# Four decoder layers on one core: expert products in groups of four within 8 steps of a scan, its lead 24 steps instead of 32, and the masks and scatters of a retrieval's tile 0 between its last picks

## What is computed

```python
# layer 1
h_new = (1-z)*n + z*h                      # GRU, 256 steps
base_out = h @ W_base.T + b_base           # _L1_ffn_ref
expert_idx = argmax(softmax(h @ router_W.T))
delta = ((h @ A) * onehot) @ Bw
x = x + base_out + delta * SCALING
# layer 2: drive = x
i_couple = tanh(q) @ coupling.T            # four times a step, each from the one before
q_next, p_next = _rk4_step(q, p, drive, coupling, bias)
# retrieval, per token, 8 heads, 8 of 4096 experts each
z = einsum('btd,bthkd->bthk', h, down_embed[indices])
z = silu(z * softmax(sc))
out = einsum('bthk,bthkd->btd', z, up_embed[indices])
x = x + out
```

## Time and profile before

| | |
|---|---|
| median of 3 runs | 5199.05 us (5195.85 to 5218.25) |
| profiled execution | 5227.58 us, span 5225.8 us |
| TensorE busy | 4851.0 us, 93% of the span |
| VectorE busy | 2831.0 us, 54% |
| ScalarE busy | 1520.9 us, 29% |
| GpSimd busy | 280.7 us, 5% |
| scan | about 966 to 2990 us of the span |
| retrieve_experts | about 2990 to 4410 us |

### The profile page before, as it was taken

How to read it: one execution, slowest core, us unless ns; L and a number is a source line. 1 busy time by engine, 2 the same in 40 slices (tenths; PEclk the granted TensorE clock), 3 DMA queues, 4 the chain that set the end, 5 groups by cost and what they waited for, 6 DMA issues and landing times. The chain is left out here.

```text
span 5225.8 us, 196853 instructions
## 1 busy us (share of the span) xinstructions
PE 4851.0 (93%) x83712; PEld 3836.6 (73%) x83712; DVE 2831.0 (54%) x16413; ACT 1520.9 (29%) x6006; POOL 280.7 (5%) x859
## 2 busy tenths in 40 slices
PE   7899999799999999999996699999989998999978
PEld 3344654589999999999996588799889997344433
DVE  3211011379999999999997635675544341444411
ACT  1100111234444444444443223233322221333310
POOL 0010010001111111111111000000000000000000
PEclk7699999655555555555555599999989999899989
DMA  2201431000000000000001000033400000000000
GB/s 80 101 34 41 165 140 35 14 4 5 5 5 5 5 5 5 5 5 5 5 5 51 13 9 2 34 87 93 128 14 3 3 3 34 11 16 17 12 21 32
DMA packets 54335, 163.72 MB, mean 31 GB/s; under 512 B 13873, under 2 KB 18097, under 8 KB 48192
## 3 DMA queue, kind: packets, MB, share of 16 engines
q1 hardware_dynamic: 47456, 134.89, 7.7%
q0 software_dynamic: 3712, 12.29, 0.7%
q10 hardware_dynamic: 2304, 4.20, 0.2%
HBM read 129.63 MB, written 17.17 MB: 28 GB/s over the span
## 5 line engine op out<-in xcount | busy, mean ns | idle before, releaser
L616 PE MATMUL k_ps<-k_hl,k_wlo 128*128 128x8 f16 x16384 | 606.6, 169 | 141.0 <-ACT k_hl L692 135.9
L616 PEld LDWEIGHTS k_ps<-k_hl,k_wlo 128*128 128x128 f16 x16384 | 532.9, 105 | 178.2 <-ACT k_hl L692 160.6
L620 PE MATMUL k_ps<-k_hl,k_whi 128*128 128x16 f16 x16384 | 588.6, 174 | 0.0
L620 PEld LDWEIGHTS k_ps<-k_hl,k_whi 128*128 128x128 f16 x16384 | 516.1, 104 | 0.6
L616 PE MATMUL g_ps<-g_hl,g_wlo 128*128 128x8 f16 x12288 | 436.7, 168 | 43.2 <-DVE g_hl L770 38.2
L620 PE MATMUL g_ps<-g_hl,g_whi 128*128 128x16 f16 x12288 | 441.5, 174 | 0.0
L616 PEld LDWEIGHTS g_ps<-g_hl,g_wlo 128*128 128x128 f16 x12288 | 387.1, 104 | 49.4 <-DVE g_hl L770 43.6
L692 ACT ACTIVATE k_hl<-k_q 128x32 f16<-128x32 f32 x768 | 176.2, 229 | 742.9 <-DVE k_q L727 742.9
L620 PEld LDWEIGHTS g_ps<-g_hl,g_whi 128*128 128x128 f16 x12288 | 387.1, 104 | 0.0
L1441 DVE TENSOR_REDUCE t_NM<-t_ps 128x1 f32<-128x512 f32 x256 | 165.1, 686 | 218.2 <-PE t_ps L1310 218.2
L1213 DVE TENSOR_TENSOR HQ<-p_ior,p_pm 128x2048 f32<-128x2048 f32 x64 | 146.3, 2290 | 223.7 <-PE p_sim L1037 223.7
(11 more groups left out here) (326 smaller groups left out, 8960.7 us busy)
## 6 DMA issues: line engine op xcount, KB each, us to landing
GRZ<-expert_places SPq DMA_DIRECT2D x64, 512.0 KB, 4.9
wm<-in_w_dram SPq DMA_DIRECT2D x4, 2816.0 KB, 10.4
GRZ<-in_w_dram SPq DMA_DIRECT2D x4, 2816.0 KB, 9.8
m_w<-in_w2a_dram SPq DMA_DIRECT2D x8, 1280.0 KB, 12.7
GRZ<-in_ue_dram SPq DMA_DIRECT2D x8, 1024.0 KB, 8.4
XT<-in_xT_dram SPq DMA_DIRECT2D x1, 4096.0 KB, 12.5
GRZ<-in_x_nat_dram SPq DMA_DIRECT2D x4, 1024.0 KB, 18.8
expert_rows<-wm SPq DMA_DIRECT2D x1, 4096.0 KB, 23.7
```

Of the source, the lines that this page charges most:

```text
L616: T.matmul(P[:,j,1,:],lo[:,kc,(m0+j)*128:(m0+j+1)*128],x[:,kc,0,:],start=(j==0 and kc==0),stop=False,skip_group_check=True)
L620: i=T.matmul(P[:,j,:,:],hi[:,kc,(m0+j)*128:(m0+j+1)*128],x[:,kc,:,:],start=False,stop=kc==KC-1,skip_group_check=True)
```

## The change

In `scan`, LEAD becomes 24. The expert work of a chunk lies in the steps i = 0 to 7: all four products with 136 columns at i = 0, four base products a step at i = 1 to 4, the transposition at i = 2, the mask at i = 3, the four low-rank products at i = 5, the additions at i = 6 and 7. NE is TL*NB, still 128, so sizes don't change. In `retrieve_experts`, the weights of tile 0 are built behind pick tile 12, its first mask behind tile 13, its other three between the products of tile 15, in buffers of their own (B0: parts of wm, R and HF). Its scatters stand behind the picks of tile 15, and ScalarE's copies of them too. The masks of tile 1 come in the order 1, 2, 3, 0, then its weights. In the last phase, combine (0,q) now stands ahead of scatter (1,q); from tile 1 on the order is as before.

```diff
-LEAD, TL = 32, 16
+LEAD, TL = 24, 16
...
-                if i<2:
-                    if i==0:
-                        e.wait_ge(g_h,TL*(j+1))
-                        if j==0: e.wait_ge(s_lw,64)
-                    for d in (2*i,2*i+1):
-                        x=T.matmul(psh[:,0:136],hs[:,d,:],ar[:,d,:],start=d==0,stop=d==3)
-                    if i==1: x.then_inc(l_h,1)
-                if i==2: e.wait_ge(l_x,4*j)
-                if 2<=i<10:
-                    for u in (2*(i-2),2*(i-2)+1):
-                        dc,d=u//4,u%4
-                        T.matmul(pso[:,dc*128:(dc+1)*128],wb[:,d,dc*128:(dc+1)*128],hs[:,d,:],start=u==0,stop=False,skip_group_check=True)
-                if i==4:
+                if i==0:
+                    e.wait_ge(g_h,TL*(j+1))
+                    if j==0: e.wait_ge(s_lw,64)
+                    for d in range(4):
+                        x=T.matmul(psh[0:NE,0:136],hs[:,d,:],ar[:,d,:],start=d==0,stop=d==3)
+                    x.then_inc(l_h,1)
+                if i==1: e.wait_ge(l_x,4*j)
+                if 1<=i<5:
+                    dc=i-1
+                    for d in range(4):
+                        T.matmul(pso[:,dc*NE:(dc+1)*NE],wb[:,d,dc*128:(dc+1)*128],hs[:,d,:],start=dc==0 and d==0,stop=False,skip_group_check=True)
+                if i==2:
                     e.wait_ge(l_ht,j+1)
...
-                if i in (10,11):
+                if i==5:
...
-                if i!=5 or j<0 or j>=NT//TL: return
+                if i!=3 or j<0 or j>=NT//TL: return
...
-                elif i in (12,13):
-                    dc=2*(i-12)+part
+                elif i in (6,7):
+                    dc=2*(i-6)+part
...
+        B0=[x.rearrange('p (j r) -> p j r',r=128) for x in (wm[:,4096:6144],R[:,0:2048],R[:,2048:4096],HF[:,0:2048])]
...
                     dense(i+1,2*q)
                     pick(i,q)
                     dense(i+1,2*q+1)
+                    if i==NTL-1: scatter(0,q)
...
-            for q in range(4): scatter(0,q)
             for i in range(NTL):
                 for q in range(4):
-                    scatter(i+1,q)
+                    if i>=1: scatter(i+1,q)
                     combine(i,q)
+                    if i==0: scatter(1,q)
...
                     if q==1 and i>=1: weight(i-1)
+                    if i==NTL-1: spread(0,q)
...
-                if i>=1: e.wait_ge(s_W,n-3)
-                else: e.wait_ge(s_t,4*NTL-3+q)
+                if i==0 and q>=1: e.wait_ge(s_t,4*NTL-3)
+                if i==1: e.wait_ge(s_t,4*NTL)
+                if i==1 and q==0: e.wait_ge(s_W,4)
+                if i>=2: e.wait_ge(s_W,n-3)
...
                     rows_hot(4*i+4+q)
+                    if i==NTL-1 and q<3: pairs_hot(q+1)
...
-            for q in range(4): pairs_hot(q)
-            weights_hot(0)
-            for q in range(3): pairs_hot(4+q)
+                if i==NTL-4: weights_hot(0)
+                if i==NTL-3: pairs_hot(0)
+            for q in range(1,4): pairs_hot(4+q)
+            pairs_hot(4)
             weights_hot(1)
-            pairs_hot(7)
```

More of the change, by code:

```diff
@@ L591, in scan @@
         view=lambda P: P[:,0:64].rearrange('p (m s b) -> p s m b',m=KC,s=2)
-        R_,Z_,N_=range(3)
+        R_,Z_,N_=range(3); NE=TL*NB
         a,h=DT/2,DT
@@ L632, in experts @@
                 hs=HS[:,j%2].rearrange('p d t b -> p d (t b)')
-                if i<2:
-                    if i==0:
-                        e.wait_ge(g_h,TL*(j+1))
-                        if j==0: e.wait_ge(s_lw,64)
-                    for d in (2*i,2*i+1):
-                        x=T.matmul(psh[:,0:136],hs[:,d,:],ar[:,d,:],start=d==0,stop=d==3)
-                    if i==1: x.then_inc(l_h,1)
-                if i==2: e.wait_ge(l_x,4*j)
-                if 2<=i<10:
-                    for u in (2*(i-2),2*(i-2)+1):
-                        dc,d=u//4,u%4
-                        T.matmul(pso[:,dc*128:(dc+1)*128],wb[:,d,dc*128:(dc+1)*128],hs[:,d,:],start=u==0,stop=False,skip_group_check=True)
-                if i==4:
+                if i==0:
[10 more added lines that the diff above has]
+                if i==2:
                     e.wait_ge(l_ht,j+1)
-                    T.transpose(pst[:,0:128],ht[:],K.ident[:]).then_inc(l_tr,1)
-                if i in (10,11):
+                    T.transpose(pst[:,0:NE],ht[0:NE,:],K.ident[0:NE,0:NE]).then_inc(l_tr,1)
+                if i==5:
                     e.wait_ge(l_hm,j+1)
-                    for dc in (2*(i-10),2*(i-10)+1):
-                        x=T.matmul(pso[:,dc*128:(dc+1)*128],bw[:,dc*128:(dc+1)*128],hm[:],start=False,stop=True,skip_group_check=True)
-                    if i==11: x.then_inc(l_o,1)
+                    for dc in range(4):
+                        x=T.matmul(pso[:,dc*NE:(dc+1)*NE],bw[:,dc*128:(dc+1)*128],hm[:,0:NE],start=False,stop=True,skip_group_check=True)
+                    x.then_inc(l_o,1)
             for s in range(LEAD):
@@ L680, in masked @@
                 j,i=s//TL-1,s%TL
-                if i!=5 or j<0 or j>=NT//TL: return
-                e.wait_ge(l_tr,j+1); A.activation(hm[:],pst[:,0:128],ACT.Copy,scale=2.0).then_inc(l_hm,1)
+                if i!=3 or j<0 or j>=NT//TL: return
+                e.wait_ge(l_tr,j+1); A.activation(hm[:,0:NE],pst[:,0:NE],ACT.Copy,scale=2.0).then_inc(l_hm,1)
             scaled(0)
@@ L777, in experts @@
                 if j<0 or j>=NT//TL: return
-                if i==2 and part==0:
+                if i==1 and part==0:
                     e.wait_ge(l_h,j+1)
-                    at['mx']=ch.did(V.tensor_reduce(mx[:],psh[:,128:136],AX.X,ALU.max))
-                elif i==2:
[L782 to L787, removed]
+                    at['mx']=ch.did(V.tensor_reduce(mx[0:NE,:],psh[0:NE,128:136],AX.X,ALU.max))
+                elif i==1:
+                    ch.after(at['mx'])
+                    at['mk']=ch.did(V.scalar_tensor_tensor(mk[0:NE,:],psh[0:NE,128:136],mx[0:NE,0:1],io[0:NE,:],ALU.is_ge,ALU.mult))
+                elif i==2 and part==0:
+                    ch.after(at['mk'])
+                    at['ix']=ch.did(V.tensor_reduce(ix[0:NE,:],mk[0:NE,:],AX.X,ALU.min))
+                elif i==2:
                     ch.after(at['ix'])
-                    V.scalar_tensor_tensor(ht[:],io16[:],ix[:,0:1],psh[:,0:128],ALU.is_equal,ALU.mult).then_inc(l_ht,1)
-                elif i in (12,13):
-                    dc=2*(i-12)+part
+                    V.scalar_tensor_tensor(ht[0:NE,:],io16[0:NE,:],ix[0:NE,0:1],psh[0:NE,0:128],ALU.is_equal,ALU.mult).then_inc(l_ht,1)
+                elif i in (6,7):
+                    dc=2*(i-6)+part
                     e.wait_ge(l_o,j+1)
                     x=XT[:,dc,:,j*TL:(j+1)*TL].rearrange('p b t -> p t b')
-                    V.scalar_tensor_tensor(x,pso[:,dc*128:(dc+1)*128].rearrange('p (t b) -> p t b',b=NB),bb[:,dc:dc+1],x,ALU.add,ALU.add).then_inc(l_x,1)
+                    V.scalar_tensor_tensor(x,pso[:,dc*NE:(dc+1)*NE].rearrange('p (t b) -> p t b',b=NB),bb[:,dc:dc+1],x,ALU.add,ALU.add).then_inc(l_x,1)
             e.wait_ge(s_c,32)
@@ L1036, in scatter @@
                         for h in range(2):
-                            x=T.matmul(psw[b][n%2][h*64:(h+1)*64,j*32:(j+1)*32],Bp[b*64:(b+1)*64,q,j,h*64:(h+1)*64],AW[b*64:(b+1)*64,q*16+j,:],start=True,stop=True)
+                            hot=B0[q] if i==0 else Bp[:,q]
+                            x=T.matmul(psw[b][n%2][h*64:(h+1)*64,j*32:(j+1)*32],hot[b*64:(b+1)*64,j,h*64:(h+1)*64],AW[b*64:(b+1)*64,q*16+j,:],start=True,stop=True)
                 x.then_inc(s_W,1)
@@ L1125, in _ @@
             weight(NTL-1)
-            for i in range(NTL):
+            for i in range(1,NTL):
                 for q in range(4): spread(i,q)
```

2 lines of the change are left out of this document (1 added, 1 removed).

## The result

| | kernel before | changed kernel |
|---|---|---|
| first comparison, median (4 runs each) | 5204.41 us | 5258.64 us (5233.91 to 5262.4) |
| ratio after / before, 95% interval | | 1.0089 (1.0056 to 1.0123) |
| second comparison, median | 5210.65 us (17 runs) | 5245.88 us (6 runs) |
| ratio, 95% interval | | 1.0068 (1.0051 to 1.0084) |
| profiled execution, span | 5225.8 us | 5231.3 us |

The changed kernel is slower, by 35 us in the better measured comparison (5245.88 - 5210.65). The forecast was 5226 us with a range of 5201 to 5242; both medians lie above it. Beside the four runs of the first comparison a fifth of the changed kernel, 5247.78 us, is on record; the ratio of that comparison, 1.0089, is lower than the ratio of its two medians, 1.0104.

A forecast was written before the change was run, and what follows sets the result against it. The recurrence TensorE, VectorE, ScalarE, TensorE was taken to bound the scan. Scan +41.1 us (72.7 + 1.8 - 34.1 + 0.7) and turn -14 us made +27 us on the median 5199.05: 5226 us, range 5201 to 5242.

The forecast's parts named there:

- The bursts: Scan, four products at a time: +4.85 us a chunk, +72.7 us beside evaluations and +1.8 us in steps of gates alone.
- The lead: Scan, lead of 24 steps: eight fewer steps of gates alone, -34.1 us, and eight tail steps with gates, +0.7 us.
- GpSimd's wait at L710: Scan: L710 showing waits for L793, the additions, was named as a sign of being wrong; the wait was costed at nothing.
- The turn: Retrieval, from picks to scatters: -19.8 us before the clock's 6 us, so -14 us, bounds -20 and -8.
- four picks, four scatters: Turn, tile 15: alternating picks at 1.97 us and scatters at 2.00 us, from 3771.28 to near 3787.8.
- wait for the weights of tile 1: Turn, ahead of scatter (1,0): TensorE waits 5.2 us while VectorE builds four masks and two weights until 3802.4.
- wait for the weights of tile 2: Turn, ahead of scatter (2,0): directly behind scatter (1,3), weights rebuilt only then, a new wait of 4.7 us.
- clock, all of it: Turn: clock falls after three idle times, each costing 2.5 us; two fall surely, the third at even chances: 6 us.
- (a): Scan: rival that dense bursts lift TensorE to 2.4 GHz, part 1 costs nothing, 5152 us; chance 0.05.
- (b): Scan: rival that the late evaluation is partly absorbed, 0.3 us in each of 90 steps, 5207 us; chance 0.07.
- (c): Retrieval: rival that the turn gives nothing, through waits and a low clock or later masks, 5240 us; chance 0.06.
- (d): Scan: rival that GpSimd's wait becomes late by 0.5 us for 15 chunks, 5234 us; chance 0.06.

## Why the prediction was right and where it was wrong

**The bursts: right.** The hop of 2.27 us, the eight instructions of 1.85 us and the missing idle time are as forecast. Of the 75.2 us, some 1.5 lie in the steps of gates alone (the first 23 of them take 99.5 us in the changed kernel, 98.0 in the kernel before; 1.8 was forecast), so a chunk costs (75.2 - 1.5) / 15 = 4.91 us; 4.85 was forecast, with bounds of 4.6 and 5.05. What I had taken off, 0.03 us for each late evaluation, is mostly not there: the quarter behind a burst takes 1.82 us, as it already did behind two products, and not the 1.79 of the tail.

**The lead: right.** 32.8 us for eight steps against 33.4, and 9.8 for two against 8.4 by the same price, (34.1 - 0.7) / 4. GpSimd's wait at L710 came, which the prediction had named as a sign of its being wrong: 378.8 us in 16 times in the changed kernel, the longest of them the prologue's 287.7, so 6.1 us in each later chunk. That sign was badly chosen. The wait says that the input is made late, not that somebody waits for it; what would have shown harm is the scan's length, and it held.

**The turn: the waits mostly right, the clock's part wrong in size and in what brings it about.** By the prediction's own steps, from pick 0 of tile 15 to the first scatter of tile 2:

| step | forecast | changed kernel |
|---|---|---|
| four picks, four scatters | 16.5 | 28.3 |
| wait for ScalarE's copies | 2.1 | 2.04 |
| combine (0,0) | 7.4 | 10.3 |
| wait for the weights of tile 1 | 5.2 | 0.77 |
| four scatters, three quarters | 30.2 | 30.1 |
| wait for the weights of tile 2 | 4.7 | 4.74 |
| clock, all of it | 6 | (in the rows above and below) |
| scatter (2,0), combine (1,0), above full clock | | 3.7 |
| sum | 72.1 | 80.0 |

The step that failed is the sentence that costs a pick at 1.97 and a scatter at 2.00 us and lets the clock fall only after idle times. Both prices come from places where the clock was full: the picks from tile 15 of the kernel before, directly behind dense products, the scatter from between two quarters of combine. In the changed kernel the granted clock was 0.5 from 3797.9 to 3832.0, and the fall came with no idle time since the 1.13 us ahead of pick 0, a wait that the kernel before has at this place too and kept 1.00 behind. The four picks and four scatters cost 28.3 - 16.5 = 11.8 us more than forecast, 11.1 of them the clock's and 0.7 idle time inside a pick and a scatter; with 2.9 in combine (0,0) and 3.7 at the end that is 18.4 in all. 4.4 of it came back, since VectorE's weights for tile 1 were less late for a slow TensorE (0.77 us of wait for 5.2). Net 14.0 in place of 6: the 8 us by which the turn gave 6 and not 14. Dense products between picks and scatters kept the clock at 1.00, with the same wait ahead of pick 0: that the missing dense work is what leaves the clock low is shown by that run. What sets the moment of the fall is not: in the five profiles of the turn without filler it came 2.4 to 9.5 us after the start of pick 0. In all five the clock came back only inside combine (0,0), 3 to 6 us after its start, and never during the picks and scatters.

The trace of the kernel before had the hint. Its four picks, then its four scatters, both without dense products between them:

```profile
3771.28:3780.62 9.34, 8.06 (x256) 7.81 (x256) 5.42 (x6) 0.26 (x1) 0.00 (x0) 1.00 0.98 396
3797.32:3812.10 14.78, 14.29 (x512) 14.03 (x512) 6.88 (x3) 5.95 (x6) 0.00 (x0) 0.50 0.01 3
```

The picks, straight behind dense work, still had the full clock for 9.34 us. The scatters began at the low one and stayed there: 97% busy for 14.78 us (14.29 of them), they took 3.7 us each and did not bring it back. And in the earlier trace rows the last window, TensorE 100% busy with scatters and the first products behind them, reads 0.50; I read that as the aftermath of the 16.70 us.

**The sum and its base.** The stages give 41.9 - 6.6 = +35 us where the forecast had +27; the 8 are the turn's. The rest of the miss is not the mechanism's. I added to 5199.05, a median of three runs; over 17 and 23 runs the kernel before has 5210.65 and 5209.42. From the first of these the same +27 would have given 5238, and +35 gives the measured 5246. In the first comparison, 5258.64 lies 33 us above the forecast: 8 are the turn's, 5 the base (5204.41), and some 19 stay open, as said above. The profiled execution at 5227.6 had said that single executions lie far apart, and the range should have carried the spread of the base too.

**The rivals.** (a), a lifted clock in the scan, falls: 0.50 in every scan measured. The Trainium skill, "TensorE: Matmul & The Clock Gate", Part 1, has the throttled state as the default that activity releases. The traces agree as far as they go: the scan's bursts did not release it (0.50), and with the filler's dense products it stayed released (1.00 over 31.48 us). (b), a partial absorption, falls with 4.91 us a chunk. (c), a turn that gives nothing, falls with -5.6 and -6.6 us, though the low clock that it named took over half of the gain. (d) falls: GpSimd waits and nobody waits for it. The chance of 0.50 for slower by over 0.5% was the largest, and 1.0068 is on that side.

## What to carry over

Where a recurrence bounds a stage, its slots can be filled to the brim and no further: work moved from twelve full slots into six costs its whole length, here 75 us, and a shorter lead bought with it (33 us) must be weighed against that; the lead that needs no bursts gave 10 us in the stage for nothing. Here a gap filled with thin work (picks and scatters, small products) did not keep the clock: before such products are costed at a duration from a dense place, ask what stands beside and ahead of them there, and look for a place in the trace where they run for long by themselves. And take the base of a forecast from as many runs as there are, and give its spread to the range.

## What was not expected of the hardware

- TensorE at 97% busy over 28.3 us, with picks and scatters of 64 and 128 instructions, was granted 0.54; with dense products between them, at 96% busy (30.17 of 31.48 us), 1.00. In this kernel the busy share in the profile does not tell the clock.
- The kernel before held 1.00 through its four picks in a row (9.34 us), and the changed kernel had lost it 2.4 us after its pick 0; between the picks of tile 15 and combine (0,0) it did not come back in any of the profiles that had lost it.
- Two stages that no edit touched vary between executions: the attention of layer 0 takes 163 us or 176 to 179 (mean clock 0.70 and 0.62 in the rows above), that of layer 3 583 to 599 (0.98 and 0.95). What decides it was not found.
- TensorE idles inside pick 1 of tile 15 for 0.18 to 2.98 us with nothing that the profile shows as a cause (0.18 and 2.75 in two executions of the same changed kernel, 2.85, 2.71 and 2.98 in the variants, 1.3 with the filler). In the run with the turn alone the DMA engines were busy throughout it (share 1.01 from 3757.10 to 3759.97); they were nearly as busy in the picks ahead of it (0.96), so whether this is the cause stays open.
